# Sorting of tokens strewn over 30 steps with four operations fewer, rows read back into the buffer of k, scatters that last into the next pass

## The reference, cut to what matters

```python
# layer 1: per image, over its 2304 tokens
xh, z = split(gn(x) @ W_in);  xc = depthwise_conv3x3(xh)
h = exp(dt_t * A) * h + (dtN_t * B_t) * x_t          # the scan, 256 x 16 states
y = sum_n(h * C_t) + Dskip * x_t
x = x + (layernorm(y) * silu(z)) @ W_out + b_out
# layer 2: q, k, v of the normalised rows; k: softmax over tokens, q: over features
context = k^T v;  t = t + layernorm((q context) @ w_out)
# layer 3: each token to its two best experts
top_logits, top_idx = top_k(ln(t) @ Wg, 2);  top_w = softmax(top_logits)
out = sum_e C_e * (silu(u W1_e) * (u W3_e + b3_e)) @ W2_e
t = t + out
```

## Time and profile before

| | us |
|---|---|
| median of 3 runs | 3913.13 (3910.83 to 3918.53) |
| the profiled execution | 3908.72 |
| its span in the trace | 3906.9 |

### The profile page before, as it was taken

How to read it: one execution, slowest core, us unless ns; L and a number is a source line. 1 busy time by engine, 2 the same in 40 slices (tenths; PEclk the granted TensorE clock), 3 DMA queues, 4 the chain that set the end, 5 groups by cost and what they waited for, 6 DMA issues and landing times.

```text
span 3906.9 us, 68984 instructions
## 1 busy us (share of the span) xinstructions
PE 3163.4 (81%) x17390; PEld 2012.8 (52%) x17390; DVE 2983.4 (76%) x5234; ACT 2553.7 (65%) x6158; POOL 2909.4 (74%) x3055
## 2 busy tenths in 40 slices
PE   5687888778889888988889887988889888776772
PEld 3233354335556555655556555655556555566662
DVE  3698989988898888878897788888898788822110
ACT  3455677457867777676867777676867777665451
POOL 1465757686769886888868897888968887966755
PEclk9788999789989998999989999999989999988896
DMA  3965656465869677886869677886869677856773
GB/s 89 221 146 129 157 124 162 120 161 137 221 177 263 153 211 197 222 221 163 233 178 244 158 208 194 231 212 162 231 185 260 157 202 195 235 150 182 241 233 109
DMA packets 420323, 730.02 MB, mean 187 GB/s; under 512 B 56203, under 2 KB 313814, under 8 KB 417750
## 3 DMA queue, kind: packets, MB, share of 16 engines
q1 hardware_dynamic: 302422, 484.13, 49.7%
q10 hardware_dynamic: 99072, 203.47, 17.0%
q0 software_dynamic: 18432, 37.93, 3.5%
HBM read 596.93 MB, written 100.07 MB: 178 GB/s over the span
## 4 chain that ended last, share of the span: by engine, by line
PE 24%; POOL 22%; issue 21%; DVE 15%; ACT 11%; DMA 4%; ACTq 2%; SPq 1%; POOLq 1%; DVEq 0%; PEldq 0%
POOL prod L698 10%; DVE state L1582 6%; PE ps_conv L901 5%; PE ps_main L967 4%; DVE ps_x L1569 3%; POOL got L821 3%; PE ps_g L1085 2%; DMA dt_rep<-dt_dram 2%; POOL rows_in L798 2%; PE ps_g L1092 2%; POOL hidden L810 2%; PE ps_y L981 2%; ACT dt_rep L1206 2%; PE ps_h L1073 2%; PE ps_x L915 1%
## 5 line engine op out<-in xcount | busy, mean ns | idle before, releaser
L698 POOL TENSOR_TENSOR prod<-state,c_rep 128x384 f32<-128x384 f32 x1536 | 1532.7, 1007 | 608.5 <-DVE state L1582 588.7
L1582 DVE TENSOR_TENSOR_SCAN state<-dt_rep,carry,ps_x 128x384 f32<-128x384 f32 x1280 | 1285.8, 1005 | 0.0
L1569 DVE TENSOR_TENSOR ps_x<-ps_x,db_rep 128x384 f32<-128x384 f32 x1536 | 852.9, 555 | 243.0 <-PE ps_x L915 223.7
L1206 ACT ACTIVATE dt_rep<-dt_rep,vecs 128x384 f32<-128x384 f32 x1536 | 917.8, 615 | 137.9 <-DMA dt_rep<-dt_dram 77.7
L915 PE MATMUL ps_x<-x_stack,copy 96*128 96x384 bf16 x1536 | 534.2, 350 | 310.8 <-DVE state L1582 306.4
L901 PE MATMUL ps_conv<-gx,w_conv 128*128 128x384 f32 x1728 | 689.6, 507 | 8.0 <-DVE parts L1599 4.6
L915 PEld LDWEIGHTS ps_x<-x_stack,copy 96*128 96x128 bf16 x1536 | 153.9, 100 | 681.6 <-DVE state L1582 493.1
L1390 ACT ACTIVATE g_sb<-ps_g,w_down 128x128 f32<-128x128 f32 x1032 | 304.2, 371 | 231.1 <-PE ps_g L1092 226.3
L901 PEld LDWEIGHTS ps_conv<-gx,w_conv 128*128 128x128 f32 x1728 | 301.1, 195 | 216.6 <-issue 129.6
L1073 PE MATMUL ps_h<-u_t,w_up 128*128 128x128 f32 x2064 | 327.5, 298 | 104.0 <-DVE silu L1799 80.0
L810 POOL TENSOR_TENSOR hidden<-g_sb,silu 128x384 f32<-128x384 f32 x344 | 343.7, 999 | 83.9 <-ACT u_out L1396 74.8
(11 more groups left out here) (256 smaller groups left out, 4958.7 us busy)
## 6 DMA issues: line engine op xcount, KB each, us to landing
dt_rep<-dt_dram SPq DMA_DIRECT2D x384, 768.0 KB
w_up<-in_w_exp ACTq DMA_DIRECT2D x344, 384.0 KB
w_down<-in_w_exp ACTq DMA_DIRECT2D x344, 193.5 KB
x_stack<-parts SPq DMA_DIRECT2D x576, 48.0 KB
u_in<-rows_in SPq DMA_DIRECT2D x344, 64.5 KB
rows_out<-u_out SPq DMA_DIRECT2D x344, 64.0 KB
dt_dram<-dt SPq DMA_DIRECT2D x192, 96.0 KB
qv<-in_x SPq DMA_DIRECT2D x48, 192.0 KB
```

Source lines behind the costliest of these rows:

```text
L698: pool.tensor_tensor(prod[:, k % HS, :], state[:, k % HS, :], c_rep[:, c % 2, :], ALU.mult).then_inc(s_prod.sem, 1)
L1206: act.activation(dt_rep[:, g % XS, q, :], dt_rep[:, g % XS, q, :], ACT.Exp, scale=decay_rate).then_inc(s_decay.sem, 1)
L1569: dve.tensor_tensor(x_n, x_n, db_rep[:, c % 2, :], ALU.mult).then_inc(s_inflow.sem, 1)
L1582: dve.tensor_tensor_scan(state[:, k % HS, :], dt_rep[:, g % XS, q, :], ps_x[k % XB][:, 0:T], init, ALU.mult, ALU.add).then_inc(s_state.sem, 1)
```

## The change

The sort's parts stand at steps 134, 136, 143, 146, 149, 152, 154, 156, 158, 161 and 164 where they stood at 132, 133 and 136 to 144; `ranks` moves from 135 to 140. Four operations of it go: the cast of the indices (they are compared as they are), one of three that make the weight, and two scalings that become part of the operation behind them (`scalar_tensor_tensor`). The scatters stand at 168 to 202 in every second step, and after the weights' copy at 207 at steps 208 to 239: 12 before k = 0 of the next pass, 24 at k = 0 to 47. The rows are read back into `k_tok`, the buffer of k, so SP waits for the sort's end and not for the scatters; the first write of `ek` to `u_tok` waits for the scatters instead. In the last pass image 6's tiles begin 16 steps later (`ENDED`), and all behind the scatters 22 steps.

```diff
-T_CHOSEN, T_RANK, T_SORT = 132, 135, 136
+T_CHOSEN, T_RANK = (134, 136), 140
+T_SORT = (143, 146, 149, 152, 154, 156, 158, 161, 164)
...
-T_SCATTER = tuple(146 + 15 * k // 8 for k in range(NT)) + tuple(183 + 15 * k // 8 for k in range(NT))
-T_SCATTER_LAST = tuple(146 + k for k in range(NT)) + tuple(165 + k for k in range(NT))
-T_HOLD, SOONEST = T_GATHER[0] - 1, 264
-ENDED, SPREAD, RESUMED = 34, T_SCATTER_LAST[0], T_SCATTER_LAST[-1] + 8
+T_SCATTER = tuple(168 + 2 * k for k in range(NT)) + tuple(208 + 15 * k // 8 for k in range(NT))
+T_SCATTER_LAST = tuple(T_SCATTER[0] + k for k in range(NT)) + tuple(T_SCATTER[0] + 19 + k for k in range(NT))
+ENDED, SPREAD, RESUMED = 50, T_SCATTER_LAST[0], T_SCATTER_LAST[-1] + 8
+T_HOLD, SOONEST = T_GATHER[0] - 1, T_W + SC - (RESUMED - 3)
...
-                    due(sp, s_scatter, m, 0)
+                    due(sp, s_sorted, m, 0)
...
-                    sp.dma_start(u_tok, image_rows(t1_dram, m)...
+                    sp.dma_start(k_tok, image_rows(t1_dram, m)...
...
                 elif kind == "ek":
                     if g == 0:
-                        act.wait_ge(*full(m, "xnT5"))
+                        due(act, s_scatter, m, 0)
...
-                    normalise(m, 0, t - T_NORM, u_tok, u_tok)
+                    normalise(m, 0, t - T_NORM, k_tok, k_tok)
...
                 if n == 4:
-                    tie(m, dve.tensor_copy(place[:, :, :], where[:, :, :]))
                     for k in range(TOP):
-                        ins = dve.tensor_tensor(chosen[k], place[:, :, k]...
+                        ins = dve.tensor_tensor(chosen[k], where[:, :, k]...
...
-                    tie(m, dve.tensor_scalar(gw[:, 1, :], gw[:, 0, :], 1.0, None, ALU.add))
-                    tie(m, dve.reciprocal(gw[:, 2, :], gw[:, 1, :]))
+                    tie(m, dve.tensor_scalar(gw[:, 1, :], gw[:, 0, :], 2.0, 2.0, ALU.mult, ALU.add))
                 if n == 7:
-                    tie(m, dve.tensor_scalar(u_weight, gw[:, 2, :], 0.5, None, ALU.mult))
+                    tie(m, dve.reciprocal(u_weight, gw[:, 1, :]))
...
-                tie(m, dve.tensor_scalar(tally[:, 3, :], counts[:, NE * NT:NE * NT + NE], 1.0 / P, None, ALU.mult))
-                tie(m, dve.tensor_tensor(picked[:, :, :], tally[:, 3, :]...
+                tie(m, dve.scalar_tensor_tensor(out=picked[:, :, :], in0=counts[:, NE * NT:NE * NT + NE]...
...
-                tie(m, dve.tensor_scalar(tally[:, 3, :], tally[:, 3, :], float(P), None, ALU.mult))
-                tie(m, dve.tensor_tensor(rank[:, :, :], counts[:, 0:NE * NT]...
+                tie(m, dve.scalar_tensor_tensor(out=rank[:, :, :], in0=tally[:, 3, :]...
```

More of the change, by code:

```diff
@@ L994, in attend @@
                     for k in range(TT):
-                        ins = pe.transpose(o[:, P * k:P * k + P], u_tok[:, TT * g + k, :], eye[:, :])
+                        ins = pe.transpose(o[:, P * k:P * k + P], k_tok[:, TT * g + k, :], eye[:, :])
                 elif kind == "kT":
@@ L1664, in route @@
                 if n == 4:
-                    tie(m, dve.tensor_copy(place[:, :, :], where[:, :, :]))
                     for k in range(TOP):
-                        ins = dve.tensor_tensor(chosen[k], place[:, :, k].unsqueeze(1).broadcast_to([P, NE, NT]),
+                        ins = dve.tensor_tensor(chosen[k], where[:, :, k].unsqueeze(1).broadcast_to([P, NE, NT]),
                                                 iota[:, 0:NE].unsqueeze(2).broadcast_to([P, NE, NT]), ALU.is_equal)
@@ L1701, in count_experts @@
                 dve.wait_ge(*read(m, "rank"))
-                tie(m, dve.tensor_scalar(tally[:, 3, :], counts[:, NE * NT:NE * NT + NE], 1.0 / P, None, ALU.mult))
-                tie(m, dve.tensor_tensor(picked[:, :, :], tally[:, 3, :].unsqueeze(2).broadcast_to([P, NE, NT]),
-                                         iota[:, 0:NT].unsqueeze(1).broadcast_to([P, NE, NT]), ALU.is_gt))
+                tie(m, dve.scalar_tensor_tensor(out=picked[:, :, :], in0=counts[:, NE * NT:NE * NT + NE].unsqueeze(2).broadcast_to([P, NE, NT]),
+                                                scalar=1.0 / P, in1=iota[:, 0:NT].unsqueeze(1).broadcast_to([P, NE, NT]),
+                                                op0=ALU.mult, op1=ALU.is_gt))
             def sum_experts(m):
@@ L1711, in place_experts @@
                 tie(m, dve.tensor_tensor(tally[:, 3, :], tally[:, 2, :], tally[:, 1, :], ALU.subtract))
-                tie(m, dve.tensor_scalar(tally[:, 3, :], tally[:, 3, :], float(P), None, ALU.mult))
-                tie(m, dve.tensor_tensor(rank[:, :, :], counts[:, 0:NE * NT].rearrange("p (e t) -> p e t", e=NE),
-                                         tally[:, 3, :].unsqueeze(2).broadcast_to([P, NE, NT]), ALU.add))
+                tie(m, dve.scalar_tensor_tensor(out=rank[:, :, :], in0=tally[:, 3, :].unsqueeze(2).broadcast_to([P, NE, NT]), scalar=float(P),
+                                                in1=counts[:, 0:NE * NT].rearrange("p (e t) -> p e t", e=NE),
+                                                op0=ALU.mult, op1=ALU.add))
             def place_rows(m, k):
@@ L1772, in attention @@
                         places(m, first, last)
-                if t in (T_CHOSEN, T_CHOSEN + 1):
-                    route(m, 4 + t - T_CHOSEN)
-                if t == T_SORT:
+                if t in T_CHOSEN:
+                    route(m, 4 + T_CHOSEN.index(t))
+                if t == T_SORT[0]:
                     route(m, 6)
-                if t == T_SORT + 1:
+                if t == T_SORT[1]:
                     count_experts(m)
-                if t == T_SORT + 2:
+                if t == T_SORT[2]:
                     sum_experts(m)
-                if t == T_SORT + 3:
+                if t == T_SORT[3]:
                     place_experts(m)
-                if t == T_SORT + 4:
+                if t == T_SORT[4]:
                     route(m, 7)
-                if t in (T_SORT + 5, T_SORT + 6):
-                    place_rows(m, t - T_SORT - 5)
-                if t == T_SORT + 7:
+                if t in T_SORT[5:7]:
+                    place_rows(m, T_SORT.index(t) - 5)
+                if t == T_SORT[7]:
                     place_tiles(m, before_m)
-                if t == T_SORT + 8:
+                if t == T_SORT[8]:
                     place_last(m)
```

4 lines of the change are left out of this document (2 added, 2 removed).

## The result

The changed kernel takes 3966.26 us in the median (3965.58 to 3968.01), the kernel before 3913.61 in the same runs: a ratio of 1.0134 (95% interval 1.0116 to 1.0151), 53 us slower where 23 us faster were forecast. Its profiled execution took 3966.45 us (span 3964.6), 57.7 more than the one of before.

The account below looks back on a forecast made before the run. DVE was taken to bound the dense sort, PE steps 144 to 167, and POOL the stretch before the subtraction from q. -51 + 27 - 4 + 5 = -23 us gave a median of 3890; 8 in 10: 3858 to 3921.

Parts of the forecast that it names:

- I take a gain of 9: Steps 128 to 167, sort spread over 30 steps: 9 us gained per full pass, 45 in five, 51 with second and eighth.
- 95% as busy as at its densest: Steps 128 to 167: with DVE as busy as in its densest 16 steps, the stretch takes 92.0 us.
- PE's clock would stay up: Steps 144 to 167, where the sort's work goes: PE's granted clock stays at 1.00.
- DVE bounds: Steps 128 to 143 of the seventh pass: DVE, busy 45.3 of 47.5 us (95%), sets the time.
- 2.8 us of DVE in each of seven passes.: Sort: four removed operations save 2.8 us of DVE per pass, or 1.2 left if another operation inherits the wait.
- POOL comes to the subtraction 5.4 us later: First subtraction from q, k = 56: seven scatters at 36 to 47 lengthen five passes by 5.4 us each, +27.
- Rival 2: POOL's queue is on the path with all it gets: 10.7 us in five passes, 10 in the last; 3925, chance 0.10.
- The six scatters at 25 to 34: Steps k = 25 to 34: six scatters (7.1 us) find cover, as POOL waits there for DVE and ACT.
- Two scatters fewer before k = 24: ACT's wait for POOL's statistics: 1 us won in each of four passes from the fifth on, -4.
- Reading back into the buffer of k: SP no longer stops for the scatters' landing; loads were covered, and ACT's `ek` wait at k = 55 counts 0.
- The last pass, "+5": Last pass: eight scatters at 34 to 47 leave POOL 5.5 us late; together +5, ends -4 and +10.
- Rival 4: Sort's two-input DVE operations wait longer where POOL is busier: 2 us a pass, 11 or 12 in all; 3901, chance 0.10.

## Why the prediction was wrong, point by point

*"I take a gain of 9" in steps 128 to 167, 51 us in all.* This step failed: the term had the wrong sign, and the stretch cost 15 us instead. It rested on two readings:

- "95% as busy as at its densest" took DVE's share over a stretch as a thing that can be kept. What can be hidden depends on the four steps. The 8.3 us of idle time counted in steps 144 to 167 lie in 144-147, 152-155 and 164-167; the sort's parts at 149, 156, 158 and 161 stood in the others. Moved into the idle fours they cost 27 us less, into the busy ones 14 more. Shown. "PE's clock would stay up" failed as well: 1.00 in steps 144 to 167 before, 0.85 in steps 164 to 167 now, some 7 us.
- "DVE bounds" in steps 128 to 143 was half of the truth. PE's waits in steps 140 to 147 of the sixth pass of the kernel before:

```profile
2439.93 0.34 PE L915 MATMUL ps_x<-x_stack,copy 96*128 96x384 bf16 x1 [1.67 <-DVE state L1582]
2442.16 2.93 PE L967 MATMUL ps_main<-xc,w_c 128*128 128x384 f32 x4 [1.90 <-DVE y L1644]
```

  PE's work there is 10.37 + 11.20 us; with these waits that fills the two windows of 24.5 (25.1 by the sum, as the ends of matmuls are modelled). As changed it works 9.70 + 13.10 us and waits 3.70 in the two windows of 26.5. DVE gave up 4.1 us in steps 140 to 147, but PE waits for it as long as before, at `ranks`, which waited 1.0 us for its bank at step 135, and has 1.2 us more work, most of it `ranks`. So the four steps 140 to 143 are as long as before and the next four 2.0 longer, while steps 132 to 139 of this pass did shrink, by 5.4 us for 5.8 of DVE's work. That PE's work and waits are what holds steps 140 to 147 is read from these rows and not shown by a run: neither a higher clock nor `ranks` a step later let them shrink, and what would wasn't found. That part is open.

So the best spread sort (3939) is 5 us behind the dense one (3934), a difference within the intervals: no spreading that was tried wins anything here.

*"2.8 us of DVE in each of seven passes."* The removed operations' own durations were added up, but part of them was waiting that others took over: alone they are worth 1.75 us of work and 1.5 to 1.9 of time in a full pass. The prediction had put 1.2 for that case and trusted the move to step 152, which held: DVE's work in the changed stretch is 87.5 us.

*"POOL comes to the subtraction 5.4 us later", +27.* The mechanism was right, the size wrong: +40 (steps 34 to 63 of five passes), and at steps 48 to 55, not at the sum of q. Of the 5.4 us of idle time I took 2.9 as cover. But of the 4.7 us that the earlier trace rows give as waits for DVE, 3.31 lie ahead of the window:

```profile
2640.23 1.00 POOL L698 TENSOR_TENSOR prod<-state,c_rep 128x384 f32<-128x384 f32 x1 [3.31 <-DVE state L1582]
```

Inside it POOL waits for DVE 1.4 us, all of it by step 41; the run with four among the gathers found 0.7 of cover. Rival 2 (10.7 in five passes) was nearer; the 5.1 a pass at which it has the change worth nothing should be 23 / 5 = 4.6. The six scatters at 25 to 34 did find cover, as said: the changed kernel's steps 24 to 33 are 2.3 to 2.9 us shorter in the last four passes, though 2.6 longer in the fourth.

*"Two scatters fewer before k = 24", -4.* Right in kind, too small: steps 24 to 33 of these four passes give -11, and all passes together with steps 0 to 23 -8. ACT's first root waits 0.43 us in the seventh pass. The run with four scatters behind the statistics gives the full price: 2.7 us a pass.

*"Reading back into the buffer of k" at 0.* The `ek` wait for the scatters doesn't show, as forecast: the first evacuation into the scatters' buffer in the seventh pass starts 8 us behind the last scatter and waits 0.38 us, and for PE.

*The last pass, "+5".* +11: all eight scatters count. The first subtraction from q starts 90.6 us behind the last scan, 81.2 before: 9.4 later, which is 8 x 1.18, and from there to the end it takes 412.2 us, 410.6 before, so nothing gives it back. The forecast had let 3.96 us of idle time absorb a part.

*Rival 4, operations that wait longer at the shared port.* DVE's work over the stretch came out at 87.5. The waits moved from one operation to another: the last multiplication of the weights takes 1007 ns in the seventh pass, before 854:

```profile
L1680 DVE TENSOR_TENSOR gw<-big_u,gw 128x18 f32<-128x18 f32 x1 | 1.0, 1007 | 0.0
```

Others wait less, and the sort's operations without the four removed take 11.07 us there instead of 11.37. So rival 4 is out as a sum, for POOL as busy as it is here (57.6 of 106.8 us). The Trainium skill (SBUF — State Buffer, "Who interferes with whom") has a DVE instruction with two SBUF inputs contend with a GpSimd instruction that reads SBUF. The trace agrees as far as such a multiplication changes its length with its place, but it doesn't tell which of POOL's instructions it waited for.

## What to carry to other kernels

Before work is spread over steps, look at each step's own bound, in windows as fine as the alternation of the work: an average over eight steps hid that DVE was full in every second four. A full four can also leave PE waiting and cost it its clock in the next. An in-order engine's spare time counts only where nothing that is waited for stands close behind; the four scatters that are free at k = 29 to 33 cost 2.7 us a pass at 17 to 22 and 4.0 at 38 to 46. When an operation is removed, ask which part of its duration was waiting, and what will wait in its stead. And where two engines are both near the path, read the second's work and waits before the first is relieved.

## What the runs showed of the hardware

PE's granted clock (its share of full speed; the two levels are 1.2 and 2.4 GHz) counts where PE is busy throughout: the same 59 matmuls of steps 164 to 167 took 9.7 us at 1.00 and 11.3 at 0.85, and the lower share stood behind four steps in which PE was busy 4.97 of 9.80 us or 7.23 of 9.80 in the sixth pass. Thirteen additional matmuls in PE's waits raised it from 0.66 to 0.82 in steps 136 to 139 of the seventh pass, which then took 9.40 us instead of 10.00; in the sixth it rose from 0.69 to 0.82 and the same steps took 0.5 us longer. An indirect scatter holds POOL for 1.01 us with a gap of 0.17, and where it is paid, the pass is longer by 1.0 (four among the gathers) to 1.3 us (8.9 for seven, with six more ahead of them) for each. An operation of DVE beside POOL's 1.81 us `rectify` can last as long as that: 1.74 us for a scaling that takes 0.17 elsewhere, and 1.87 for the operation that inherited it and takes 0.31 elsewhere.
